# Graph attention layer: where TensorE turns a group's rows and turns them back, among its sums and scores

## The reference, cut to what matters

```
h = (x @ gat_W).reshape(n, H, C1)
a_src = jnp.einsum('nhc,hc->nh', h, att_src)
a_dst = jnp.einsum('nhc,hc->nh', h, att_dst)
logits = jax.nn.leaky_relu(a_src[src] + a_dst[dst], negative_slope=0.2)
alpha = _segment_softmax(logits, dst, n)
msg = h[src] * alpha[:, :, None]
x1 = jax.ops.segment_sum(msg, dst, num_segments=n).reshape(n, H * C1) + gat_bias
x1 = _prelu(x1, prelu1_a)
```

## Time and profile before

| | us |
|---|---|
| median of 3 executions | 4656.9 |
| lowest and highest | 4648.12, 4657.92 |
| span of the profiled execution | 4657.7 |
| the attention layer's 52 groups in it | about 2329 to 3477 |

### The profile page before, as it was taken

One profiled execution on the slowest core, in us unless ns is written; L12 is line 12 of the kernel. 1 busy time (PEld: TensorE's weight loads), 2 busy tenths in 40 slices (PEclk: granted clock), 3 DMA queues, 4 the chain that ended last, 5 costly groups with the idle time before them and its releaser, 6 DMA issues. The chain is left out here.

```text
span 4657.7 us, 73581 instructions
## 1 busy us (share of the span) xinstructions
PE 3535.7 (76%) x14587; PEld 2519.3 (54%) x14588; DVE 2670.9 (57%) x10225; ACT 741.8 (16%) x2298; POOL 3229.3 (69%) x3404
## 2 busy tenths in 40 slices
PE   2366666666566666666588888988887989999988
PEld 2244444444344444444366666666665766766766
DVE  8544444444333444344377777877776766766765
ACT  3200000000011111111011111111111223222222
POOL 3477777777677777777677776767627777766762
PEclk7687778778798999898878888888888999999999
DMA  5544444444444444444455555555425555555552
GB/s 163 137 130 129 131 131 129 129 131 132 114 138 136 137 136 139 139 138 134 120 149 150 149 147 140 147 140 145 137 73 143 162 152 153 159 143 151 153 145 82
DMA packets 339366, 639.85 MB, mean 137 GB/s; under 512 B 85419, under 2 KB 218598, under 8 KB 338790
## 3 DMA queue, kind: packets, MB, share of 16 engines
q0 software_dynamic: 159744, 440.25, 35.4%
q1 hardware_dynamic: 159993, 180.48, 12.2%
q10 hardware_dynamic: 19056, 12.87, 1.0%
HBM read 569.33 MB, written 63.99 MB: 136 GB/s over the span
## 5 line engine op out<-in xcount | busy, mean ns | idle before, releaser
L582 POOL DMA_INDIRECT g_G<-t,srcI x1664 | 1587.6, 954 | 507.2 <-issue 507.2
L755 PE MATMUL g_ps<-g_G,g_oh 128*128 128x256 f32 x3328 | 1030.9, 460 | 479.6 <-DMA g_G<-t,srcI 392.9
L755 PEld LDWEIGHTS g_ps<-g_G,g_oh 128*128 128x128 f32 x3328 | 725.5, 228 | 749.1 <-issue 418.8
L881 POOL DMA_INDIRECT g_G<-t,srcI x832 | 806.1, 969 | 302.2 <-issue 247.2
L1471 POOL DMA_INDIRECT g_G<-t,srcI x832 | 793.5, 954 | 291.5 <-issue 252.1
L1812 PE MATMUL g_psA<-g_win,g_ohT 128*128 128x257 f32 x1664 | 546.6, 413 | 104.1 <-issue 58.8
L1573 DVE CUSTOM_DVE_ANT_0 g_junk<-g_G,g_psA 128x257 f32<-128x257 f32 x832 | 348.1, 418 | 290.4 <-PE g_psA L1812 265.2
L1822 PE MATMUL g_ps<-g_G,g_oh 128*128 128x257 f32 x1664 | 508.2, 389 | 0.0
L1245 PE MATMUL g_ps<-g_Gp,g_oh 128*128 128x264 f32 x1664 | 451.1, 424 | 47.6 <-issue 26.1
L636 DVE TENSOR_SCALAR g_oh<-iota,g_relx,g_wx 128x128 f32<-128x128 f32 x1664 | 452.1, 364 | 53.3 <-PE g_ps L755 29.4
L1812 PEld LDWEIGHTS g_psA<-g_win,g_ohT 128*128 128x128 f32 x1664 | 293.2, 197 | 211.5 <-issue 84.8
(11 more groups left out here) (293 smaller groups left out, 3880.3 us busy)
## 6 DMA issues: line engine op xcount, KB each, us to landing
g_G<-t,srcI POOLq DMA_INDIRECT x3328
g_relb<-relrow SPq DMA_DIRECT2D x104, 512.0 KB, 5.6
g_own<-t SPq DMA_DIRECT2D x159, 128.0 KB, 2.2
t<-g_t SPq DMA_DIRECT2D x53, 132.0 KB, 2.7
g_rec<-t SPq DMA_DIRECT2D x53, 132.0 KB
g_rec<-h SPq DMA_DIRECT2D x53, 128.5 KB, 2.6
x<-g_o SPq DMA_DIRECT2D x53, 128.5 KB, 2.8
g_rec<-x SPq DMA_DIRECT2D x53, 128.5 KB, 2.7
```

What stands on the lines that cost most here:

```text
L582: pool.indirect_dma_start(G[:, b, u, :], None, table, IOA(ap=m.srcI[:, g * UW + u:g * UW + u + 1], axis=0)).then_inc(s_g[b][u // QW], 16)
L755: last = nc.tensor.matmul(ps[:, 0:D], oh[:, u, :], G[:, b, u, :], start=(u == 0), stop=(u == UW - 1))
L881: pool.indirect_dma_start(G[:, b, u, :], None, m.t3, IOA(ap=m.srcI[:, g * UW + u:g * UW + u + 1], axis=0)).then_inc(s_g[b], 16)
```

## The change

In TensorE's body, and nowhere else, three pieces change places. R moves from behind the third quarter of the sums to behind the first. The other three quarters follow it in one run. B moves from behind the scores to ahead of them. The fillers stay ahead of the node's turn, now behind the scores. The number of instructions and every semaphore value stay the same. The fillers are L1284 in the new text, R is L1269 and L1270, B L1277 and L1278.

```
                 if agg:
-                    for q in range(3):
-                        add(q)
+                    add(0)
                 if logits:
                     pe.wait_ge(s_s1, k + 1)
                     hold(m, pe)
                     nc.tensor.transpose(psR[0:H, 0:P], W[:, :, 0], m.ident[:])
                     nc.tensor.transpose(psR[0:H, P:2 * P], W[:, :, UW - 1], m.ident[:]).then_inc(s_rt, 1)
                 if agg:
-                    add(3)
-                if lead:
-                    for q in range(NQ):
-                        score(k + 1, kh + (b % 2), b + 1, q)
+                    for q in range(1, NQ):
+                        add(q)
                 if logits:
                     pe.wait_ge(s_s2, k + 1)
                     hold(m, pe)
                     nc.tensor.transpose(psB[:, 0], In[:], m.ident[0:H, 0:H])
                     nc.tensor.transpose(psB[:, 1], Out[:], m.ident[0:H, 0:H]).then_inc(s_bt, 1)
+                if lead:
+                    for q in range(NQ):
+                        score(k + 1, kh + (b % 2), b + 1, q)
+                if logits:
                     for j in range(3):
                         nc.tensor.matmul(psW[:], m.ident[:], m.rows[:, 0:2, :], start=True, stop=True)
```

## The result

| | before | after |
|---|---|---|
| median (runs) | 4652.51 us (4) | 4620.11 us (4) |
| lowest and highest | 4634.7, 4657.92 | 4615.94, 4624.67 |
| ratio, 95% interval | | 0.9927 [0.9907, 0.9946] |
| span of the profiled execution | 4657.7 | 4622.7 |

The changed kernel is 34 us faster by the ratio (0.73%), 32.4 by the medians and 35.0 by the two profiled executions; the prediction said 13. Read the stage first, cut as in the earlier trace rows: from the second group to where VectorE starts the last one (L1094). Of the kernel after that is 2350.00 to 3416.50, 39.5 us less than the 1106.00 of before.

The account below looks back on a forecast made before the run. The prediction took TensorE's own row of work to set a group's length. Its terms, -18.0 (turn) + 8 (wait ahead of R) - 3 (clock) = -13 us, took 4657.7 to 4644.7, 4644 us on the median's scale; range 4622 to 4673.

Parts of the forecast that it names:

- The wait for the turn: TensorE at L1215: scores and fillers now lie between B and the node's turn, so all its waits go, -18.0 us.
- The wait ahead of R: TensorE ahead of R, behind one quarter of the sums: a new wait for the scan L1116, +8 us.
- the comparison of rings: Per group, VectorE's ring of 18.7 us against TensorE's own 17.8; up to 0.9 us of wait ahead of R.
- The clock: Attention stage on TensorE: two fewer stretches at half clock, -3 us.
- The 26.1 and 23.3 us and the 19.9 us are not touched: TensorE's waits behind branch L1254 and at the loop's end, "issue" and ahead of the first sum, stay: no gain.
- Given back: Rival, chance 0.30: the 18 us at the turn return as waits ahead of R; 4657, range 4650 to 4664.
- Slower, idling ahead of R lets the clock fall: Rival, chance 0.18: idling between the first quarter of the sums and the rest slows the sums; 4682, 4666 to 4705.
- VectorE's wait for B was on the path: Rival, chance 0.09: the 34.6 us ahead of L1153 come off with the 18; 4604 to 4630, say 4620.
- L1130 under 30: Sign of the forecast being right: VectorE's wait at scan L1130, which needs R, falls from 72.7 us to under 30.
- Waits of L967 in their place: Sign of the forecast being right: on VectorE, waits of L967 for the sums replace the wait of L1153 for B.
- R's wait 5 to 15 beyond the start: Sign of the forecast being right: TensorE's L1269 (R) waits 5 to 15 us beyond the start.
- the larger gain: Case of 4604 to 4630, chance 0.09; its sign: the mean group falls under 21.6 us from 22.1.

Follow-up runs that it names:

- B alone: Kernel before with only B moved ahead of the scores, R left behind three quarters of the sums: 4620.47 us, ratio 0.9923.
- R alone: Kernel before with only R moved behind the first quarter of the sums, B left behind the scores: 4717.40 us against 4653.64, ratio 1.0131.
- R behind two quarters: Kernel before with R moved behind two quarters of the sums and B ahead of the scores: 4620.03 us, ratio 0.9925.
- after with padding: Changed kernel with 64 never-executed instructions added inside the skipped branch L1254: 4616.69 us, ratio 0.9909 against the kernel before.

## Why the prediction was wrong

Direction right (the chance for faster was 0.46), size wrong: 4620.1 against 4644, just below the range of 4622 to 4673.

- **The wait for the turn** (-18.0): right. L1215 is gone from the waits, and B alone does nearly all of it. All idle time ahead of it is 18.0 us in the longer stretch of the earlier trace rows and 16.3 in the one compared here, and 0.0 in the kernel after:

```profile
L1215 PE MATMUL g_psN<-ident,g_t4r 128*128 128x128 f32 x100 | 20.7, 289 | 16.3 <-DVE g_t4r L1040 13.5
```

- **The wait ahead of R** (+8; bounds 0 to +46): right in kind, too small. It is 27.7 us against 2.0, +26, in 44 groups. The step that failed is the comparison of rings: "TensorE's own ring is 17.8 ... and passes 18.7 as soon as they take 3.5 us or more". However far VectorE is ahead, the scan can't start before L1100, and L1100 needs L1251, which TensorE itself issues right ahead of the sums. Rows of before had most of its price: L1100 to the scan's end 1.93 us, against 8 x 0.2325 = 1.9 for the quarter. What is left is the two handovers, which in the kernel after are 0.25 us from the first sum's start to L1100 and 0.15 from the scan to R: by that estimate some 0.4 us in nearly every group, 20 us in all. The chain was named in the prediction only as a place of VectorE's slack ("L1100, which needs L1251").
- **The clock** (-3; bounds -10 to +10): outside its bounds. Busy time fell by 18.4 us at 0.88 (17.7 at equal work). It came with R behind one quarter and B early together: R alone and B alone stay at 0.86, R behind two quarters too. The clock of whole executions says the same: 0.868 to 0.872 in all eight of the kernel after and of after with padding, 0.861 to 0.869 in thirteen of before, 0.863 to 0.865 in B alone. So the two misses on R nearly cancel, +26 and -18, and R's move is worth nothing.
- **"The 26.1 and 23.3 us and the 19.9 us are not touched"**: wrong, and this is what put the time outside the range. The prediction put them at nothing; ahead of the first sums and of L1251 TensorE idled 70.9 us and now idles 41.1: -30, of which 23.0 are the nine stalls and 6.0 are L1251 at the loop's end. The reason given, "the change leaves the same number of TensorE instructions in a group, so the branches stay where they are in the code", holds for the number of instructions, and doesn't imply what was drawn from it: with the branches where they were and another order of the work, the nine stalls were gone. The prediction named a change in these stalls as what would make it wrong, but gave it no chance.
- Sum with the measured terms, at equal work: -16.3 (turn) + 25.7 (R) - 29.8 (stalls and loop's end) - 17.7 (clock) = -38.1, the whole of what the stage lost. The execution as a whole lost 35.0, mostly since group 1 begins 2.8 us later.

The rivals. *Given back* had the price ahead of R nearer (18 us; 26 measured), but with it and the turn alone the sum is +9, 4666, just above its upper end of 4664. *Slower, idling ahead of R lets the clock fall*: its wait came in more groups than the 7 it needed, over 25 us in all, and the clock rose. The Trainium skill says (TensorE: Matmul & The Clock Gate, Part 4: PE-mode transpose) that transposes don't count as busy time of the array as matmuls do. No such loss shows here: the version with R and a wait between the first two quarters has the higher granted clock, 0.88 against 0.86. No run separates the transposes from the wait ahead of them. *VectorE's wait for B was on the path* gave 4620, the time that was measured, and for another reason: it counted the 34.6 us of L1153 as gain, but with B alone TensorE's idle time fell by 42.2 us in the places named above, all of which are in TensorE's own list, and the nine stalls among them went in R alone too, where VectorE's wait for B rose to 143.1 us.

What the profile was to show: L1130 under 30 (10.3), no wait of L1153 for B, L1215 under 2: so. Waits of L967 in their place: hardly (8.0), L1100's instead (61.7). R's wait 5 to 15 beyond the start: no, 27.7 in all and 23.6 without the first. Clock up by 0.01: 0.02. One sign was met that belonged to the larger gain: the mean group fell to 1071.0 / 50 = 21.4 us, under 21.6.

**What stays open.** How the order of the work takes the nine stalls away, and why five of L1251's at the loop's end get shorter (23.3 to 17.3 us). Transfers on the instruction queue that start 6 to 11 us ahead of L1251 stand in 13 groups of the kernel after and 18 of B alone against 8 of before; but R alone, which has no such stall either, has them in 6, and the queue serves all engines. Padding of the kernel after takes its stalls at the loop's end from 17.5 to about 5.5 us and its stage from 1071.0 to 1060.8 in the profiled executions, so there may be time left in the place of the code; by the medians, 4616.7 against 4620.1 in another set, it isn't settled. Why R behind one quarter raises the clock when B is early, and not when it is late, is open as well.

## What to carry to other kernels

A stall behind a taken branch that the profile puts down to another engine can hang on where the code lies. Never-executed instructions inside the skipped block tell: if the stalls change groups, it does, and then a change in the order of work, even one that leaves the number of instructions alone, can take them away. Price them as a term of their own, with a chance, and count all of them, the loop's end included: here the padding moved them without changing their sum.

Before moving a wait ahead of other work, look for the shortest chain from the engine's own last signal back to it: TensorE can't be served sooner than its L1251, VectorE's five instructions and two handovers allow, and what stands between must be that long, whatever the slack of the whole ring. And try the halves of a change alone: here one was the whole gain, the other alone cost 64 us, and in the other kind of set neither gained alone (+1.7% and +0.6%) while both together did (-0.7%).

## What the runs showed of the hardware that I had not expected

- Where the code lies decided which groups stalled: 2.2 to 3.1 us behind a taken branch in 9 of 50 groups of before, in 15 groups, most of them others, with 64 never-executed instructions added (2.1 to 3.2 us), and none past the loop's end with the 16 small products of the scores behind B, or with R moved.
- The same program takes 4653 us in some sets of runs and 6182 to 6236 us in others, on one chip in both; in the slower kind three engines nearly stop for about 12 us a group while GpSimd's gathers go on at one each 1.25 us.
- A wait of 0.2 to 0.7 us ahead of R in 40 of 50 groups went with a higher granted clock (0.88 against 0.86, 18 us less of busy time), not with a lower one.
